# Two recurrent attention layers with expert gates on one core: gate and routing steps split and moved, the second experts one batch later

## The chip, the cores and the metric

One NeuronCore of one Trainium2 chip runs the whole program. The metric is the time of one execution in microseconds (us), taken on the device; the kernel before was run three times. A separate execution was profiled: its trace gives every row below. Engines are PE (TensorE), DVE (VectorE), ACT (ScalarE), POOL (GpSimd) and SP (SyncE, which here only issues DMAs).

## The reference, cut to what matters

`x` is 8 batches of 512 tokens of width 128. Two layers follow each other, each adds a product of two branches to `x`:

```python
xn = layernorm(x)
s = attn0(xn)                    # two 8-head attentions on 64 columns each (one on a Holt-smoothed copy),
                                 # two layernorms, a 128-512-128 relu MLP, a layernorm
g = silu(ffn0(xn))               # 16 experts, top 1, capacity 256 tokens, 128-512-128
x = x + s * g
xn = layernorm(x)
s = attn1(xn)                    # 16 heads of 8, causal, ALiBi
g = silu(ffn1(xn))               # 8 experts, top 2, 128-256-128 gated, no capacity limit
x = x + s * g
```

Attention is per batch. An expert layer needs the routing of all 4096 tokens before the first of its expert tiles can run, and the gate `g` of any batch needs all tiles. All of it is float32, with bfloat16 pieces in the scores (queries and keys are split into three bfloat16 parts).

## The kernel before, in words

**Stages.** `normalise0` normalises all tokens and scores the first gate. Then one software pipeline, `attention`, runs over steps b = -3 to 16 (`batches`, `plan`). Step b computes scores and softmax of batch b (batches 0 to 7 are layer 0, 8 to 15 layer 1), the row maxima of batch b+1, loads and projections of batches b+2 and b+3, and what is left of batches b-1 and b-2. Two blocks of expert tiles stand between steps: `experts0` (16 tiles) at the start of b = 1, and `experts1` (40 tiles of 256 slots) at the start of b = MIX1 = 11.

**Units and places.** A step of layer 0 has 64 units, one of layer 1 has 40. A unit is one bank of scores of batch b (PE L483, three banks in a ring, ACT takes the exponential, L642 to L646) and one bank of products for the maxima of batch b+1 (PE L491, another ring of three banks, DVE reduces it, L727 to L736). So PE can be three units ahead of ACT or DVE, and no more. The units are spread over 32 places, and at each place the tables `MISC` (every batch; by layer) and `EXTRA` (named b) name further steps. All five engines walk the same list in the same order, each doing its part of a step; semaphores with counted values are the only other order. All further PE products go through one bank, `ps_misc`, which the next step may claim only when the last has been read.

**Steps the change touches.**
- `q` and `k` (places 4 and 6; 3 and 5 in layer 1): PE projects, ACT writes `whole["q"]` or `whole["k"]` (L666), POOL splits it into three bfloat16 parts (L829 to L832, four instructions), SP writes these to DRAM. ACT waits before L666 until *all* splits so far are done.
- `gather`: POOL issues 4 (layer 0) or 8 (layer 1) indirect DMAs that fetch expert rows (L868). `gate`: POOL weighs them (L877 or L879 to L881), ACT takes the tanh (L679). `mix`: DVE makes `gz` (L783), POOL multiplies with the attention result and adds `x` (L892, L893), SP stores (L439).
- `choose`, `count`, `weigh` in b = ROUTE1 = 9: the second routing on DVE, 50-odd small dependent instructions (L903 to L907, L1478 to L1515, L1523 to L1527), in two blocks with a PE product between them.
- `send` (L1552): POOL issues 64 indirect DMAs that scatter the tokens to their slots in `sent1`, 24 in b = 9, 40 in b = 10. The tiles' first loads wait for all 64.
- `experts0.send_pool(2)`, on POOL's queue at the start of b = 1, ends with a wait for the DMAs that fill `sent1` with zeros (7 MB, issued by SP behind the last expert store).
- In b = 8, the first of layer 1, batch 7 still runs its layer-0 rest: `proj` and `gather` at place 7, `ln1` at 9 (POOL L839 to L846), `yT` at 15, `ff1` from 16, `ff2` at 23, `mix` at 28.
- Layer-1 batches 8 to 15 are mixed two in b = 11, two in b = 12, and one each in b = 13 to 16; step 16 has no units.

Of the kernel before, what the change touches and what calls it, by code (L numbers as in the profile page):

```python
# [15 lines left out]
P = 128  # L16
# [113 lines left out]
MIX1 = NB + 3  # L130
# [12 lines left out]
    1: {0: [("zT", 2)], 2: [("shift", 0, 1)], 3: [("q", 2)], 4: [("norm", -1, QT - 1)], 5: [("k", 2)], 7: [("onT", -1)],  # L143
        8: [("v", 1), ("load", 3)], 12: [("norm", 0, 0)], 16: [("fetch", 2, 0)], 17: [("proj", -1)], 19: [("shift", 1, 0)], 20: [("norm", 0, 1)],
        28: [("norm", 0, 2)]},
}

EXTRA = {
    ROUTE1: {12: [("choose", 0)], 14: [("count", 0)], 15: [("send", 0, 0)], 20: [("weigh", 0)]},
    ROUTE1 + 1: {7: [("send", 0, 1)], 18: [("send", 0, 2)]},  # L150
    MIX1: {0: [("loadx", -3), ("gather", -3)], 10: [("gate", -3)], 14: [("mix", -3)],
           15: [("loadx", -2), ("gather", -2)], 26: [("gate", -2)], 30: [("mix", -2)]},
    MIX1 + 1: {0: [("loadx", -2), ("gather", -2)], 10: [("gate", -2)], 14: [("mix", -2)],
               17: [("loadx", -1), ("gather", -1)], 26: [("gate", -1)], 30: [("mix", -1)]},
    **{b: {8: [("loadx", -1), ("gather", -1)], 24: [("gate", -1)], 30: [("mix", -1)]} for b in range(MIX1 + 2, STREAM + 1)},
}
# [46 lines left out]
def plan(b):  # L203
# [13 lines left out]
    def misc(place):  # L217
        for k in range(2):
            for step in MISC[k].get(place, []):
                if live(step[1]) and layer(step[1]) == k:  # L220
                    if step[0] == "fetch":
                        fetch(*step[1:])
                    else:
                        add(*step)
# [53 lines left out]
def adds(step):  # L278
# [5 lines left out]
    if name == "fetch":  # L284
# [34 lines left out]
def attention(nc, const, psum, banks, strips, late, work, dram, weights, routes, out, experts_of):  # L319


    with ExitStack() as ctx:
# [18 lines left out]
        neg_max = sb("neg_max", [P, 2, NG, QT])  # L341
        neg_block = sb("neg_block", [P, 2, NG, QT * QT])
# [6 lines left out]
        resid = [sb(f"resid{i}", [P, QT, D]) for i in range(2)]  # L349
# [30 lines left out]
        with nc.Block() as block:  # L380

            @block.sync
            def _(sp):
                n = Tally(adds)
                for b, steps in batches():
# [4 lines left out]
                    for step in steps:  # L390
# [1275 lines left out]
```

## Time and profile before

| | us |
|---|---|
| median of 3 runs | 1276.57 (1275.53 to 1281.41) |
| profiled execution | 1285.47 |
| its span, first to last instruction | 1283.5 |
| PE busy / DVE / ACT / POOL | 1049.2 / 776.5 / 656.6 / 541.2 |
| mean granted TensorE clock | 0.926 of full |

In slices of the span a busy share of PE near 0.9 stands for both steps at full rate and stretches at half clock, so the granted clock is to be read beside it. Starts of the steps, taken as the first exponential of a batch: b = 1 at 242.6, b = 2 at 316.8, b = 8 at 708.9, b = 9 at 771.8, b = 10 at 836.8, b = 11 at 1031.5, b = 12 at 1082.5, b = 13 at 1137.3, b = 14 at 1182.9, b = 15 at 1222.0; its last exponential ends at 1256.5. The expert tiles of layer 1 run from 908.9 to about 1030.

### The profile page before, as it was taken

The page shows a single profiled execution, that of the slowest core. Times are in us where ns is not written, and L with a number is a line of the kernel's source. Part 1 is how long each engine was busy: PE and PEld are TensorE (multiplying, and loading weights), DVE is VectorE, ACT ScalarE, POOL GpSimd, SP SyncE. Part 2 cuts the span into 40 slices and gives each one's busy share as a digit, 9 for nine tenths or more (in the row PEclk, how much of TensorE's full clock was granted, in tenths as well). Part 3 has the DMA queues.
Part 4 walks back from the last instruction along what each step waited for, and adds up shares of the span by engine and source line. Part 5 has one row for each costly group of instructions (what it writes and reads, how often), then busy time and mean ns, then how long its engine had stood idle before and what let it go on. Part 6 is the DMA issues. An engine that isn't in the chain of part 4 may idle for free.

```text
span 1283.5 us, 24573 instructions
## 1 busy us (share of the span) xinstructions
PE 1049.2 (82%) x8630; PEld 544.6 (42%) x8630; DVE 776.5 (60%) x1696; ACT 656.6 (51%) x1245; POOL 541.2 (42%) x568
## 2 busy tenths in 40 slices
PE   5349889969989898988899787784699978889982
PEld 5112249623333333333334444342589944434541
DVE  6359772457878787878755646754244446557710
ACT  1000662446767666667666545353244446556672
POOL 3154400062727272737363724477100056654344
PEclk9955999989999999999999989797799989899997
DMA  6345347661414141414141415244488843433211
GB/s 180 118 124 127 85 131 211 209 148 34 105 29 106 29 103 34 108 26 116 27 117 27 117 26 151 68 123 136 115 243 249 239 121 89 111 82 87 60 35 41
DMA packets 133348, 137.60 MB, mean 107 GB/s; under 512 B 14233, under 2 KB 115193, under 8 KB 133017
## 3 DMA queue, kind: packets, MB, share of 16 engines
q1 hardware_dynamic: 127096, 123.59, 37.1%
q0 software_dynamic: 6144, 12.60, 3.8%
q8 instruction: 66, 1.08, 0.4%
q14 instruction: 42, 0.34, 0.1%
HBM read 88.11 MB, written 54.58 MB: 111 GB/s over the span
## 4 chain that ended last, share of the span: by engine, by line
PE 51%; POOL 18%; DVE 9%; issue 6%; ACT 6%; DMA 4%; SPq 1%; POOLq 0%; ACTq 0%; DVEq 0%
PE ps_banks L526 7%; PE ps_banks L491 5%; PE ps_banks L1422 5%; PE ps_banks L483 5%; POOL sent L1552 5%; POOL tokens L868 4%; DVE a_neg_max L727 4%; PE ps_banks L602 3%; PE ps_banks L1435 2%; PE ps_banks L1217 2%; PE ps_banks L1203 2%; PE ps_banks L597 2%; PE ps_banks L545 2%; PE ps_banks L502 2%; PE ps_banks L566 2%
## 5 line engine op out<-in xcount | busy, mean ns | idle before, releaser
L727 DVE TENSOR_REDUCE a_neg_max<-ps_banks 128x1 f32<-128x512 f32 x512 | 325.8, 684 | 95.2 <-PE ps_banks L491 93.3
L642 ACT ACTIVATE a_probs<-ps_banks 128x512 f32<-128x512 f32 x512 | 282.9, 598 | 142.8 <-PE ps_banks L483 140.5
L491 PE MATMUL ps_banks<-k_strip,q_strip 51*128 51x128 bf16 (+2 forms) x1536 | 299.0, 296 | 42.9 <-DMA k_strip<-k_rows 21.6
L483 PE MATMUL ps_banks<-q_strip,k_strip 53*128 53x128 bf16 (+3 forms) x1408 | 283.7, 299 | 16.8 <-DVE a_neg_max L727 6.8
L644 ACT ACTIVATE a_probs<-ps_banks 128x512 f32<-128x512 f32 x256 | 146.9, 598 | 113.6 <-PE ps_banks L483 111.0
L491 PEld LDWEIGHTS ps_banks<-k_strip,q_strip 51*128 51x128 bf16 x1536 | 101.3, 95 | 233.9 <-ACT a_probs L642 109.7
L868 POOL DMA_INDIRECT tokens<-made,at x96 | 92.9, 968 | 155.5 <-DMA made<-work 127.9
L483 PEld LDWEIGHTS ps_banks<-q_strip,k_strip 53*128 53x128 bf16 x1408 | 94.8, 95 | 123.2 <-ACT a_probs L642 52.6
L729 DVE TENSOR_REDUCE a_neg_block<-ps_banks 128x4 f32<-128x512 f32 x128 | 87.2, 689 | 95.9 <-PE ps_banks L491 94.7
L526 PE MATMUL ps_banks<-a_probs,v_aug 128*32 128x512 f32 x1024 | 140.4, 621 | 0.0
L732 DVE TENSOR_REDUCE a_neg_block<-ps_banks 128x4 f32<-128x512 f32 x128 | 83.2, 683 | 31.8 <-PE ps_banks L491 31.5
L1535 DVE SCALAR_TENSOR_TENSOR work<-ps_banks,work 128x256 f32<-128x256 f32 x80 | 35.0, 480 | 87.4 <-ACT work L1458 58.0
L829 POOL CAST a_q_parts<-a_q_whole 128x512 bf16<-128x512 f32 x16 | 9.8, 612 | 182.3 <-DMA sent<-in_zeros 100.6
L1552 POOL DMA_INDIRECT sent<-tokens,at x64 | 61.5, 962 | 45.6 <-DVE at L1515 26.5
L1422 PE MATMUL ps_banks<-work 128*128 128x256 f32 x320 | 78.9, 391 | 1.3 <-DMA work<-in_pack 1.2
L808 POOL TENSOR_SCALAR a_ff_veps<-a_ff_moments 128x4 f32<-128x4 f32 x8 | 1.9, 235 | 161.8 <-DVE a_ff_moments L701 161.8
L1458 ACT ACTIVATE work<-ps_banks,work 128x256 f32<-128x256 f32 x80 | 33.6, 471 | 58.0 <-PE ps_banks L1422 58.0
L1422 PEld LDWEIGHTS ps_banks<-work 128*128 128x128 f32 x320 | 59.4, 196 | 9.1 <-DMA work<-in_pack 1.9
L502 PE MATMUL ps_banks<-mask_kq,ident_bf 128*128 128x512 bf16 x128 | 52.2, 408 | 7.8 <-ACT a_probs L644 6.3
L508 PE MATMUL ps_banks<-mask_qk,ident_bf 128*128 128x512 bf16 x128 | 51.7, 404 | 6.6 <-DVE a_neg_block L736 5.5
L545 PE MATMUL ps_banks<-consts,a_o_strip 128*128 128x128 f32 x256 | 42.6, 290 | 14.2 <-ACT a_o_strip L649 5.8
L736 DVE TENSOR_REDUCE a_neg_block<-ps_banks 128x4 f32<-128x512 f32 x64 | 42.1, 685 | 11.3 <-PE ps_banks L491 11.3
(223 smaller groups left out, 1691.1 us busy)
## 6 DMA issues: line engine op xcount, KB each, us to landing
work<-in_pack SPq DMA_DIRECT2D x40, 450.0 KB, 3.5
q_rows<-a_q_parts SPq DMA_DIRECT2D x96, 128.0 KB
k_rows<-a_k_parts SPq DMA_DIRECT2D x96, 128.0 KB
q_strip<-q_rows SPq DMA_DIRECT2D x64, 192.0 KB
k_strip<-k_rows SPq DMA_DIRECT2D x64, 192.0 KB
work<-in_w SPq DMA_DIRECT2D x32, 256.0 KB, 3.2
sent<-in_zeros SPq DMA_DIRECT2D x14, 512.0 KB, 7.9
work<-sent SPq DMA_DIRECT2D x56, 128.0 KB, 3.2
```

The costliest lines, as they stand in the source:

```text
L483: mm = pe.matmul(sbank[:, at:at + hi - lo], k_now[rows(js, ROW_END), slot, kt * P:(kt + 1) * P], q_now[rows(js, ROW_END), slot, lo:hi], st ...
L491: mm = pe.matmul(mbank[:, at:at + hi - lo], q_next[rows(jm, ROW_SHIFT), slot, qt * P:(qt + 1) * P], k_next[rows(jm, ROW_SHIFT), slot, lo:h ...
L502: pe.matmul(sbank, ident_bf[:], const["mask_kq"][:], start=True, stop=False)
L526: mm = pe.matmul(out_of[c], v_of[k][c], probs[group % 2][:, c, :], start=k == 0, stop=k == QT - 1)
L642: act.activation(probs[si // 4 % 2][:, si % 4, :], bank, ACT.Exp).then_inc(sems["probs"], 1)
L644: act.activation(probs[e // 4][:, e % 4, :], bank, ACT.Exp).then_inc(sems["probs"], 1)
L727: dve.tensor_reduce(neg_max[:, half, hd, qt:qt + 1], bank, AX.X, ALU.max, negate=True).then_inc(sems["max_out"], 1)
L729: dve.tensor_reduce(neg_block[:, half, hd, 0:QT * QT:QT], bank.rearrange("p (t n) -> p t n", t=QT), AX.X, ALU.max, negate=True).then_inc(s ...
L732: dve.tensor_reduce(neg_block[:, half, hd, :].rearrange("p (t k) -> p t k", t=QT)[:, 2:4, 1:3], bank.rearrange("p (t k n) -> p t k n", t=2 ...
L868: pool.indirect_dma_start(rows[:, t, :], None, moe[layer], bass.IndirectOffsetOnAxis(ap=routes[layer]["at"][i][:, QT * at + t:QT * at + t ...
L1422: mm = pe.matmul(hidden_bank(par, i)[:, c, :], pack[par][:, (i * FC1 + c) * P:(i * FC1 + c + 1) * P], rows_T[par][:], start=True, stop=True)
L1552: pool.indirect_dma_start(dram["sent1"], bass.IndirectOffsetOnAxis(ap=at[i][:, t:t + 1], axis=0), xn_all[:, t, :], None).then_inc(sems["se ...
```

## The change

It edits order and waits; the arithmetic stays, except that in layer 1's last batch DVE rather than POOL multiplies and adds.

- ACT, before writing `whole["q"]` or `whole["k"]`, waits for all splits but the last one (q and k alternate, so the last one read the other buffer).
- `gate` becomes `gate` (POOL), `tanh` (ACT) and `gz` (DVE) with places of their own; `mix` leaves its store to a step `store`.
- `choose` is cut in two, what was `count` in three (`count`, `place` 1, `place` 2), spread over places 12 to 24 of b = 9; `weigh` at 27.
- Sends go in 8 pieces of 8 DMAs: b = 9 place 28, b = 10 places 7, 15, 23, 30, b = 11 places 7, 15, 23. The wait for the zero fill stands before the first piece.
- MIX1 = 12: the expert tiles come after b = 11. Batches are mixed two per step in b = 12, 13 and 14; in b = 15 batch 14 is mixed, and batch 15 is gathered, gated and `gz` made. Attention results get three buffers. In b = 12 `proj` stands at 17.
- Step 16 has `final` in place of `proj`: the product, then two DVE instructions from PSUM and SBUF, then the store.
- In b = 8 batch 7's `gather` moves to 11, behind `ln1`; `yT` to 17, `ff1` to 18 to 21, `ff2` to 24, `mix` to 30.
- `neg_max` and `neg_block` are laid out so that `minus` reads them in order.

```diff
-MIX1 = NB + 3
+MIX1 = NB + 4
-        22: [("gate", -1), ("ff2a", -1)], 23: [("ff2", -1)], 25: [("ln2", -1)], 26: [("norm", 0, 2)], 28: [("mix", -1)]},
+        22: [("gate", -1), ("ff2a", -1)], 23: [("ff2", -1)], 24: [("tanh", -1)], 25: [("ln2", -1)], 26: [("norm", 0, 2), ("gz", -1)], 28: [("mix", -1)],
+        30: [("store", -1)]},
-    1: {... 7: [("onT", -1)], ... 17: [("proj", -1)], ...
+    1: {... 7: [("onT", -1)], ... 10: [("proj", -1)], ...
+LAST0 = {
+    **MISC[0], 7: [("proj", -1)], 11: [("gather", -1), ("logits", -2)], 15: [], 16: [("fetch", 2, 0)], 17: [("yT", -1)], 18: [("norm", 0, 1), ("ff1", -1, 0)],
+    19: [("ff1", -1, 1)], 20: [("ff1", -1, 2)], 21: [("shift", 1, 0), ("ff1", -1, 3)], 22: [("gate", -1)], 23: [("ff2a", -1)], 24: [("ff2", -1)], 25: [("tanh", -1), ("ln2", -1)],
+    26: [], 28: [("gz", -1)], 30: [("mix", -1)], 31: [("store", -1)],
+}
+def mixed(d, *at):
+    names = (("loadx", "gather"), ("gate",), ("tanh",), ("gz",), ("mix",), ("store",))
...
 EXTRA = {
-    ROUTE1: {12: [("choose", 0)], 14: [("count", 0)], 15: [("send", 0, 0)], 20: [("weigh", 0)]},
-    ROUTE1 + 1: {7: [("send", 0, 1)], 18: [("send", 0, 2)]},
-    MIX1: {0: [("loadx", -3), ("gather", -3)], 10: [("gate", -3)], 14: [("mix", -3)],
-           15: [("loadx", -2), ("gather", -2)], 26: [("gate", -2)], 30: [("mix", -2)]},
-    MIX1 + 1: {0: ... -2 ..., 17: [("loadx", -1), ("gather", -1)], 26: [("gate", -1)], 30: [("mix", -1)]},
-    **{b: {8: [("loadx", -1), ("gather", -1)], 24: [("gate", -1)], 30: [("mix", -1)]} for b in range(MIX1 + 2, STREAM + 1)},
+    ROUTE1: {12: [("choose", 0, 0)], 15: [("choose", 0, 1)], 18: [("count", 0)], 21: [("place", 0, 1)], 24: [("place", 0, 2)],
+             27: [("weigh", 0)], 28: [("send", 0, 0)]},
+    ROUTE1 + 1: {7: [("send", 0, 1)], 15: [("send", 0, 2)], 23: [("send", 0, 3)], 30: [("send", 0, 4)]},
+    ROUTE1 + 2: {7: [("send", 0, 5)], 15: [("send", 0, 6)], 23: [("send", 0, 7)]},
+    **{MIX1 + i: merged(mixed(i - 4, 0, 8, 11, 13, 14, 17), mixed(i - 3, 15, 24, 27, 29, 30, 31), {17: [("proj", -1)]} if i == 0 else {}) for i in range(3)},
+    STREAM - 1: merged(mixed(-1, 0, 8, 11, 13, 14, 17), mixed(0, 18, 25, 28, 30)),
 }
...
-                            wait(act, sems["split"], n.at("split"))
+                            wait(act, sems["split"], n.at("split") - 1)
...
-                            wait(act, sems["x2"], n.at("x2"))
-                            act.activation(s1_out[par]...
+                            wait(act, sems["x2"], NB + at - 2)
+                            act.activation(s1_out[at % 3]...
...
+                        if name == "final":
+                            wait(dve, sems["misc"], n.at("misc") + 1)
+                            wait(dve, sems["gate_out"], n.at("gate_out"))
+                            dve.tensor_tensor(sg[:], ps_misc.rearrange("p (t d) -> p t d", t=QT), gz[:], ALU.mult).then_inc(sems["misc_free"], 1)
...
+                            dve.tensor_tensor(x2[:], sg[:], x_in[:], ALU.add).then_inc(sems["x2"], 1)
...
-            pool.wait_ge(sems["zeroed1"], 16 * zero_dmas(w, TILES1 * SLOTS1))
+    def zeroed_pool(pool):
+        pool.wait_ge(sems["zeroed1"], 16 * zero_dmas(w, TILES1 * SLOTS1))
```

## Rows read from the trace of the kernel before

**Rows 1.** Windows: busy us (xcount) of PE, PEld, DVE, ACT, POOL; granted clock, DMA share, GB/s.

```profile
708.90:771.80 62.90, 51.78 (x592) 28.56 (x594) 36.03 (x90) 32.13 (x58) 32.21 (x35) 0.95 0.32 73
...
771.80:836.80 65.00, 47.61 (x570) 24.83 (x570) 46.45 (x117) 29.03 (x55) 28.80 (x32) 0.87 0.44 112
836.80:882.50 45.70, 39.67 (x538) 21.07 (x530) 27.32 (x52) 26.79 (x50) 35.72 (x38) 0.96 0.55 145
882.50:908.90 26.40, 0.00 (x0) 0.00 (x1) 2.30 (x6) 1.24 (x3) 17.36 (x19) 0.55 0.23 78
908.90:1031.50 122.60, 119.99 (x734) 106.91 (x738) 51.96 (x121) 50.30 (x122) 0.00 (x0) 0.97 0.75 218
1031.50:1082.50 51.00, 41.38 (x540) 21.35 (x532) 28.66 (x52) 29.69 (x55) 31.50 (x32) 0.93 0.45 107
1082.50:1137.30 54.80, 44.01 (x549) 22.23 (x548) 30.55 (x57) 29.02 (x55) 34.18 (x34) 0.91 0.45 103
1137.30:1182.90 45.60, 41.09 (x550) 21.43 (x548) 29.44 (x55) 28.40 (x55) 20.66 (x21) 0.96 0.40 95
1182.90:1222.00 39.10, 36.68 (x541) 20.10 (x539) 29.31 (x56) 26.46 (x51) 13.57 (x13) 1.00 0.23 50
1222.00:1256.50 34.50, 29.90 (x384) 15.77 (x383) 5.33 (x15) 25.41 (x50) 13.74 (x14) 1.00 0.12 32
1256.50:1283.50 27.00, 3.97 (x40) 2.44 (x40) 1.24 (x3) 2.94 (x6) 15.86 (x15) 0.70 0.18 49
```

**Rows 2.** Windows, same columns: one PE stall, and the stretches behind three PE stalls.

```profile
258.00:266.30 8.30, 0.39 (x7) 0.09 (x3) 0.69 (x1) 0.78 (x2) 3.51 (x4) 0.65 0.91 184
266.30:272.00 5.70, 5.70 (x30) 3.78 (x30) 3.56 (x20) 2.85 (x6) 4.47 (x6) 0.61 0.45 121
...
738.90:745.00 6.10, 6.10 (x41) 2.70 (x42) 0.88 (x2) 1.29 (x3) 2.26 (x2) 0.50 0.00 0
...
804.60:810.70 6.10, 6.10 (x45) 1.95 (x45) 5.69 (x21) 1.59 (x4) 0.00 (x0) 0.56 0.01 3
```

**Rows 3.** Waits: engine line <- releaser: us in total, times, longest us.

```profile
ACT a_k_whole L666 <- POOL a_q_parts L832: 42.4, 15, 9.0
...
PE ps_banks L1409 <- DMA work<-sent: 26.4, 1, 26.4
```

**Rows 4.** Timeline of b = 1, POOL and ACT: start, us, instruction, [idle before <-releaser].

```profile
261.68 0.61 POOL L829 CAST a_q_parts<-a_q_whole 128x512 bf16<-128x512 f32 x1 [100.56 <-DMA sent<-in_zeros]
...
265.52 0.69 ACT L666 ACTIVATE a_k_whole<-ps_banks,bk 128x512 f32<-128x512 f32 x1 [9.01 <-POOL a_q_parts L832]
```

**Rows 5.** Timeline of PE, in b = 8 and in b = 11.

```profile
738.89 1.11 PE L593 MATMUL ps_banks<-consts,work 128*128 128x128 f32 x4 [4.14 <-POOL work L844]
...
1047.47 1.12 PE L582 MATMUL ps_banks<-consts,a_o_norm 128*128 128x128 f32 x4 [4.10 <-ACT a_k_whole L666]
```

**Rows 6.** Timeline of DVE in b = 9: the routing's first and last instruction.

```profile
798.66 0.42 DVE L903 TENSOR_REDUCE work<-logits 128x32 f32<-128x256 f32 x1
...
815.40 0.18 DVE L1515 CAST at<-work 128x32 uint32<-128x32 f32 x1
```

**Rows 7.** Timeline of ACT and POOL in b = 9: q, then sends 1, 24 and 64.

```profile
779.28 0.60 ACT L666 ACTIVATE a_q_whole<-ps_banks 128x512 f32<-128x512 f32 x1 [0.74 <-PE ps_banks L566]
...
816.41 1.14 POOL L1552 DMA_INDIRECT sent<-tokens,at  x1 [26.54 <-DVE at L1515]
...
845.65 0.95 POOL L1552 DMA_INDIRECT sent<-tokens,at  x1 [0.30 <-issue]
...
904.39 0.96 POOL L1552 DMA_INDIRECT sent<-tokens,at  x1 [0.30 <-issue]
```

**Rows 8.** Timeline of the end: the last PE product and the last addition.

```profile
1261.97 1.16 PE L587 MATMUL ps_banks<-wo,a_o_T 128*128 128x128 f32 x8 [0.69 <-ACT a_o_T L653]
...
1276.67 1.26 POOL L893 TENSOR_TENSOR work<-tokens,work 128x512 f32<-128x512 f32 x1
```

**Rows 9.** Source L761, a DVE addition from PSUM: count, ns least/median/most.

```profile
L761 DVE TENSOR_TENSOR tokens<-ps_banks,a_resid x8: 691/692/692, 268.4 to 724.3; 128x512 f32<-128x512 f32 x8
```

More of the change, by code:

```diff
@@ new lines, in mixed, with merged @@
+def mixed(d, *at):
+    names = (("loadx", "gather"), ("gate",), ("tanh",), ("gz",), ("mix",), ("store",))
+    places = {}
+    for place, steps in zip(at, names):
+        places.setdefault(place, []).extend((name, d) for name in steps)
+    return places
+def merged(*tables):
+    places = {}
+    for table in tables:
+        for place, steps in table.items():
+            places.setdefault(place, []).extend(steps)
+    return places
+EXTRA = {
+    ROUTE1: {12: [("choose", 0, 0)], 15: [("choose", 0, 1)], 18: [("count", 0)], 21: [("place", 0, 1)], 24: [("place", 0, 2)],
[4 more added lines that the diff above has]
+    STREAM - 1: merged(mixed(-1, 0, 8, 11, 13, 14, 17), mixed(0, 18, 25, 28, 30)),
@@ L218, in misc @@
         for k in range(2):
-            for step in MISC[k].get(place, []):
-                if live(step[1]) and layer(step[1]) == k:
+            for step in (LAST0 if b == NB and k == 0 else MISC[k]).get(place, []):
+                if not live(step[1]) or layer(step[1]) != k or step[0] == "proj" and b == MIX1:
+                    continue
+                if step[0] == "proj" and b == STREAM:
+                    add("final", -1)
+                else:
                     if step[0] == "fetch":
@@ L295, in adds @@
         "ln2": {"pool": 2, "s": 1}, "gather": {"rows": 16 * QT * (1 if layer == 0 else TOP)},
-        "gate": {"gate_in": 1, "gate_tanh": 1, "pool": 0 if layer == 0 else 1},
-        "mix": {"gate_out": 1, "pool": 1, "x2": 1, "x2_out": 16},
+        "gate": {"gate_in": 1, "pool": 0 if layer == 0 else 1}, "tanh": {"gate_tanh": 1}, "gz": {"gate_out": 1},
+        "mix": {"pool": 1, "x2": 1}, "store": {"x2_out": 16}, "final": {**both, "x2": 1, "x2_out": 16},
         "ln3a": {"dve": 1, "moments": 1, "rstd": 1, "pool": 1}, "ln3b": {"xn2": 1, "xn2_out": 16},
-        "choose": {}, "count": both, "weigh": {}, "send": {},
+        "choose": {}, "count": both, "place": {}, "weigh": {}, "send": {},
     }
@@ L1472, in linking, with choose_vector @@
         return link
-    def choose_vector(dve):
+    def choose_vector(dve, part):
         link = linking(dve)
         number = const["all"][:, C_EXP1:C_EXP1 + E1]
-        first_best(dve, link, logits[:], E1, number, best[0], flag, first, onehot[0])
-        link(dve.scalar_tensor_tensor(rest[:], onehot[0][:], MASK, logits[:], ALU.mult, ALU.add))
+        if part == 0:
+            first_best(dve, link, logits[:], E1, number, best[0], flag, first, onehot[0])
+            link(dve.scalar_tensor_tensor(rest[:], onehot[0][:], MASK, logits[:], ALU.mult, ALU.add))
+            return
         first_best(dve, link, rest[:], E1, number, best[1], flag, first, onehot[1])
@@ L1492, in place_vector, with tile_vector @@
         before, totals = (ps_misc[:, i * NT * E1:(i + 1) * NT * E1].rearrange(by_expert, e=E1) for i in range(2))
-        total = places(dve, link, last_read, before, totals, run, pos)
+        assert places(dve, link, last_read, before, totals, run, pos) is run[1]
+    def tile_vector(dve):
+        link = linking(dve)
+        total = run[1]
         link(dve.tensor_tensor(filled[:], total[:, NT - 1, :].unsqueeze(2).broadcast_to([P, E1, FILLS]),
@@ L1549, in send_pool @@
             pool.wait_ge(sems["slots"], 1)
-        for t in range(*SEND[part]):
+        for t in range(QT * part, QT * (part + 1)):
             for i in range(TOP):
```

69 lines of the change are left out of this document (39 added, 30 removed).

## The prediction

> **What bounds the kernel now.** I read the windows first, one for each step of the pipeline and each gap between stages [rows 1], and in them three things: how long the step is, how busy PE is, and what clock PE was granted. The layer-1 steps do almost the same work (the same 40 units; steps 9 to 13 also the same projections), so the best of them is a measure for the others. Step 13 takes 45.6 us with PE busy for 41.1; step 9 takes 65.0, step 11 takes 51.0 and step 12 takes 54.8. PE sets a layer-1 step where nothing disturbs it; the rest is stalls. DVE is the next engine: 29.4 us of 45.6 in step 13, but 46.5 of 65.0 in step 9, where the routing runs.
>
> Then the stretches behind stalls [rows 2]. After each stall PE runs at about half clock for some us: granted 0.61 over 5.7 us, 0.50 over 6.1 us, 0.56 over 6.1 us, that is the 1.2 GHz level instead of 2.4 for all or most of it. Work lost is (1 - clock) times length: 2.2, 3.0 and 2.7 us. So a stall of several us costs itself and 2 to 3 us more. By the same arithmetic step 13 lost (1 - 0.96) x 45.6 = 1.8 us, and an undisturbed layer-1 step is 45.6 - 1.8 = 43.8 us [rows 1].
>
> Last the waits and timelines, for what ends each stall: the zero fill (step 1), POOL's y (step 8), the splits by POOL (steps 9 to 12), the routing (step 9), the sends (before the tiles), and the gate at the end.
>
> **The change part by part.** All sums are in the profiled execution: span 1283.5, time 1285.5, against a median of 1276.6 (0.7% less).
>
> 1. *Zero fill.* In step 1 POOL's first split starts at 261.68 because it stood behind the wait for the zeros, and ACT's `k_whole` at 265.52 behind that split [rows 4]. PE is busy 0.39 us of 8.30: 7.9 lost, and 2.2 behind it at low clock [rows 2]. The wait moves in front of the first send, some 540 us later, when the zeros have long landed. POOL's other wait there, for the expert stores, stays, and the split parts are written to DRAM behind the zeros on the same queue; their readers come at place 16, twice as far into the step as place 7 where PE stood. Bounds: 0 (the stores are as late as the zeros) and 10.1. The DMA share of 0.91 in that window at 184 GB/s is the zero fill itself, not the stores, so I take 10.
>
> 2. *Own-buffer waits.* ACT waited 42.4 us in 15 places for a split [rows 3]; 9.0 are those of part 1. In layer 0 the wait is short and PE has up to three units in hand; I count nothing (bounds 0 and 3 in all). In layer 1 PE stood 4.10 us in step 11 for `k_whole` [rows 5], because POOL had put the eight gather DMAs ahead of the split; about as much in 12, half of it in 9 and 10. It is contained in the step lengths below. What is late next is POOL itself (parts 5 and 6).
>
> 3. *Step 8.* PE waits 4.14 us for y [rows 5] and then loses 3.0 at half clock [rows 2]. The four gather DMAs, 1.26 us each as the sends are [rows 7], now come after `ln1`, so y is ready about 5 us earlier and PE claims it two places later: the stall goes. In exchange `ff2` is one place later and with it the last x of layer 0, on which DVE waits at place 1 of step 9; a place is 2 us (62.9 / 32 [rows 1]), about what is gained elsewhere. Bounds 2 and 7.1; I take 6.5.
>
> 4. *Step 9, the routing.* It keeps all its instructions; only the blocks get smaller. The first block began at 798.66 and the last ended at 815.58 [rows 6], 16.9 us with three reductions in between; with `weigh` it is 17 us of DVE, as 46.5 - 29.4 says too [rows 1]. PE can be three units ahead, some 3 us. From place 12 on DVE has 17 + 20/32 x 29.4 = 35.4 us of work; PE has 20/32 x 43.8 = 27.4. So DVE bounds the rest of this step, split or not, and small blocks only fill its idle time and avoid the long PE stalls with the slow clock behind them. The routing starts at 798.7 - 771.8 = 26.9 into the step, less 4 by part 2 (2.3 of stall, 1.7 behind it): 22.9. Add 35.4, 1.2 for DVE waiting for the count product behind which `shift` at place 19 must queue, less 2.5 by which PE is ahead at the end: 57 instead of 65.0. Bounds: 52 (the whole three units are in hand each time) and 65.
>
> 5. *The sends.* The slots are known after place 24: 22.9 + 15.9 + 12/32 x 29.4 + 1.2 = 51 into the step. By parts 1 and 3 step 9 starts at 771.8 - 16.5 = 755.3, so the slots are there at 806.3, and the first eight sends run to 816.4 at 1.26 each; this pace is the same among attention work (sends 1 to 24: 29.2 us for 23 steps) and alone (to send 64) [rows 7]. Step 10 starts at 812.3. From then POOL is never free: the next sends stand behind the splits, which need `q_whole`, 8.1 us into a step (779.88 - 771.8 [rows 7]): 820.4. In steps 10 and 11 POOL owes four splits, 4 us each (265.52 - 261.68 = 3.84 [rows 4]), 16 in all, and 56 sends, 70.6: done at 907.0. Before, send 64 ended at 905.35 and PE began the tiles at 908.9; with the same 3.5 us they now begin at 910.5. Steps 10 and 11 are 43.8 each and PE is done at 899.9: it waits 10.6 us where it waited 26.4 [rows 1, 3]. The splits of step 11 stand behind send piece 5 and end about 19 us into the step; their strips are fetched at place 16, 22 us in, and PE reads them in the next step: covered, by little on SP and by far on PE.
>
> 6. *After the tiles.* They take 122.6 us [rows 1], unchanged: step 12 starts at 1033.1. Steps 12 to 15 now mix seven batches and gate the eighth. POOL's load for a step with two: 34.2 busy as in step 12 before, 16 x 0.30 us between DMAs [rows 7], two landings of under 2 us: about 43 in 43.8 us. It just fits, and since `tanh` and `gz` are 3 to 5 places behind `gate`, ACT waits at `tanh` for 1 to 3 us, which the three banks mostly cover. I take step 12 at 44 (the step behind the tiles was shorter at its start), 13 at 45.5, 14 at 40 (39.1 before), 15 at 37.5 (34.5 before; now two gathers, and POOL's second gate comes late against its short places). Bounds: nothing for the gates (43.8 + 43.8 + 39.1 + 34.5 = 161.2) and what steps 11 and 12 showed (rival one); mine sum to 167.0.
>
> 7. *The end.* PE's last product ends at 1263.13 and the last addition at 1277.93 [rows 8]; between them lie gather, landing, gate, tanh, gz and mix. Now two DVE instructions of 0.69 [rows 9] follow the product: 1264.7, 13.2 less. From the last exponential to the end that is 27.0 - 13.2 = 13.8. It needs `gz` of batch 15 before that, for which step 15 has room. Bounds 9 and 13.5.
>
> 8. *Layout of the maxima, three result buffers, places in layer 0.* Two DVE instructions in a half get contiguous reads; DVE isn't the bound there. Nothing (bounds -2 and +2).
>
> The sum: 1033.1 + 167.0 + 13.8 = 1213.9, against 1283.5: **69.6 us less**. By source: zeros 10, step 8 6.5, step 9 8, step 10 1.9, wait for the sends 15.8, steps 11 to 13 18 (151.4 becomes 43.8 + 44 + 45.5 = 133.3), steps 14 and 15 -3.9, end 13.2. Profiled time 1285.5 - 69.6 = 1215.9, a factor of 0.946; on the median 1276.6 that is 1207.5.
>
> **A rule that speaks against it.** Of the 64 sends, 24 were issued beside attention with DVE at work, at 1.27 us, and the other 40, half of them with DVE idle, at (904.39 - 845.65 - 8 for the two splits between) / 40 = 1.27 [rows 7]. So DVE's work here costs the sends nothing. The Trainium skill says otherwise for some work ("SBUF — State Buffer", SBUF: two separate sides): a DVE instruction in a two-port mode locks GpSimd out, which then can't write the descriptors of its DMAs, 3.1 us against 0.62 in its example. By that rule more sends beside attention would be slower; the same page, under Who interferes with whom, exempts reductions, and by that the trace agrees. It is the last rival, priced from rows.
>
> **The rivals.**
>
> *One: the gates keep costing what they did.* For: steps 11 and 12 held two mixes each and took 51.0 and 54.8, and PE stood for `tanh` in both; POOL's 43 us of 43.8 leave nothing, so any lateness is carried on. Against: of their excess the larger part is the wait for the split, which goes, and `tanh` stood at the very place of `gate`. Then step 12 is 51.0, 13 is 54.8, 14 is 39.1 + 5, 15 is 34.5 + 9: 193.4 in place of 167.0, in all 1234.
>
> *Two: POOL is done in time and PE doesn't wait for the sends.* For: the wait is 10.6 us in a sum of 100 us, and a longer step 10 or 11 hides part of it; if the routing ends 5 us sooner, the sends do too. Against: POOL's sum has no guess in it but the slots' time. Then 10.6 less: 1197.
>
> *Three, on the other side: sends beside attention are slow.* All 56 that follow the first piece lie on POOL's chain to the tiles, now beside projections, splits and their DMAs. At x us each the end moves by 56 (x - 1.26): the gain is used up at x = 2.5, a time of 1277, and at 3 us each it is 1305. For it: nothing but that POOL's DMAs now share two whole steps with the rest. Against it: the even pace of both kinds of send [rows 7].
>
> *Four: the change doesn't take effect.* If a moved wait stands in the path again (the expert stores, `x2` before `loadx` on SP's queue), single terms of the sum fail, 10 to 20 us each; all of them don't.
>
> **How the numbers follow.** My forecast: 0.67, with a range of its own of 1198 to 1219 (parts 3, 4 and 6 by their bounds, not all at once). Rival one 0.15, rival two 0.10, three 0.03, four 0.05 (1220 to 1245). What a measurement of this kernel tells from no change is about 0.5%, 6 us. Faster 0.95, same 0.02, slower 0.03. The range 1195 to 1236 holds the first three cases; some 0.15 is left out.
>
> **What would show it.** In the profile after: PE busy through step 1 without the 7.9 us hole; step 8 near 56; step 9 near 57 with DVE busy about 46 of it, no PE stall over 2 us and a clock over 0.93; 64 sends at 1.26, the last about 907; a hole of about 10 us before the tiles (none: rival two; over 30: rival three); steps 12 and 13 at 44 to 46, with ACT waiting 1 to 3 us at the tanh (over 50: rival one); about 14 us from the last exponential to the end. I am wrong if step 9 stays at 65, if the pace of the sends changes, or if steps 12 to 15 sum to over 180.

## The result and the profile after

The changed kernel takes 1216.74 us (median of 4 runs, 1212.89 to 1225.2); the kernel before, run beside it, took 1278.99 (1275.53 to 1282.14). The ratio is 0.952, interval 0.946 to 0.959. The forecast was 1207.5, range 1195 to 1236: right in sign and about 9 us too low. Two further series gave 0.950 [0.948, 0.952] and 0.954 [0.949, 0.958]. Two single runs, of after_again at 1635.95 us and of last0_undone at 1597.63, had a mean granted clock of 0.56 and 0.64, and their medians below are those of the other three runs.

Windows of the profiled execution after (span 1223.4, time 1225.2), columns as in [rows 1]: step 1, steps 8 to 11, the hole before the tiles, the tiles, steps 12 to 15, the end. The tiles now stand behind step 11.

```profile
242.30:306.60 64.30, 56.72 (x368) 20.36 (x367) 49.13 (x102) 43.75 (x82) 29.96 (x30) 1.00 0.54 146
...
695.60:755.30 59.70, 52.30 (x592) 28.53 (x594) 34.83 (x90) 32.26 (x59) 29.52 (x33) 0.94 0.34 77
755.30:816.10 60.80, 48.87 (x566) 25.77 (x562) 45.69 (x118) 29.08 (x55) 21.30 (x24) 0.86 0.42 107
816.10:858.90 42.80, 39.44 (x552) 21.13 (x548) 28.50 (x53) 27.83 (x52) 30.00 (x33) 1.00 0.47 119
858.90:900.30 41.40, 38.45 (x538) 20.56 (x531) 27.64 (x53) 26.58 (x50) 32.87 (x36) 1.00 0.59 160
900.30:913.60 13.30, 0.00 (x0) 0.00 (x0) 2.32 (x6) 1.25 (x3) 7.67 (x8) 0.65 0.28 97
913.60:1033.70 120.10, 118.45 (x734) 105.84 (x738) 51.91 (x120) 50.26 (x121) 0.00 (x0) 0.98 0.75 223
1033.70:1081.80 48.10, 41.57 (x540) 21.36 (x539) 28.61 (x51) 29.67 (x55) 31.45 (x32) 0.93 0.46 114
1081.80:1129.00 47.20, 41.27 (x549) 21.31 (x548) 31.77 (x57) 28.89 (x55) 34.09 (x34) 0.96 0.48 114
1129.00:1169.60 40.60, 37.31 (x541) 19.99 (x540) 32.62 (x59) 27.03 (x52) 28.04 (x27) 1.00 0.32 74
1169.60:1209.50 39.90, 34.20 (x384) 17.69 (x383) 5.36 (x14) 26.00 (x51) 26.18 (x26) 0.85 0.20 54
1209.50:1223.40 13.90, 7.09 (x40) 4.20 (x40) 1.93 (x4) 1.66 (x3) 0.00 (x0) 0.50 0.07 19
```

The profiled execution is 8 us above the median, so the table sets a second profile of the same kernel (*after_3*, span 1215.2) beside it. Lengths are compared, not instants: what lies ahead of step 1 varied by 7 us from run to run (step 1 starts at 242.3 and at 235.0). The last column is the best version of the experiments. All in us.

| stretch | before [rows 1] | forecast | after | after_3 | best |
|---|---|---|---|---|---|
| step 8 | 62.9 | 56.4 | 59.7 | 56.7 | 56.7 |
| step 9 | 65.0 | 57 | 60.8 | 61.5 | 61.6 |
| steps 10, 11 | 45.7, 51.0 | 43.8, 43.8 | 42.8, 41.4 | 42.8, 41.4 | 42.8, 41.4 |
| hole before the tiles | 26.4 | 10.6 | 13.3 | 13.3 | 1.7 |
| tiles | 122.6 | 122.6 | 120.1 | 120.2 | 118.1 |
| steps 12 to 15 | 54.8, 45.6, 39.1, 34.5 | 44, 45.5, 40, 37.5 | 48.1, 47.2, 40.6, 39.9 | 47.7, 47.3, 40.7, 40.7 | 45.6, 44.8, 40.3, 32.9 |
| end | 27.0 | 13.8 | 13.9 | 13.9 | 14.8 |
| sum from step 8 | 574.6 | 515.0 | 527.8 | 526.2 | 500.7 |

Ahead of step 8 the change took off 13.0 us: 9.9 in step 1 (74.2 to 64.3) and 3.1 in steps 2 to 7 (392.1 to 389.0), of which only the first was forecast. From step 8 on the forecast was 11 to 13 us too low, most of it in steps 12 to 15. So the total was nearer than its terms, since gains that nobody had booked, 3.1 us in layer 0 and 2.5 in the tiles, cover part of the misses: that part is luck.

Two waits carry it (columns as in [rows 3]). The first answers to the 26.4 of [rows 3]; the second is ACT standing before the tanh until POOL has formed the gate's input.

```profile
PE ps_banks L1453 <- DMA work<-sent: 13.3, 1, 13.3
...
ACT tokens L710 <- POOL tokens L921: 11.4, 5, 3.5
```

The same in the timelines (columns as in [rows 4]): the first split of step 1, which answers to [rows 4]; the last of the 64 sends; the tanh in step 12; the last product and addition, which answer to [rows 8].

```profile
253.26 0.61 POOL L869 CAST a_q_parts<-a_q_whole 128x512 bf16<-128x512 f32 x1 [94.54 <-ACT a_q_whole L697]
...
909.15 0.96 POOL L1605 DMA_INDIRECT sent<-tokens,at  x1 [0.31 <-issue]
...
1057.62 0.63 ACT L710 ACTIVATE tokens<-tokens 128x512 f32<-128x512 f32 x1 [3.54 <-POOL tokens L921]
...
1217.12 2.07 PE L617 MATMUL ps_banks<-wo,a_o_T 128*128 128x128 f32 x8 [0.69 <-ACT a_o_T L684]
...
1219.95 0.69 DVE L823 TENSOR_TENSOR work<-tokens,work 128x512 f32<-128x512 f32 x1
```

The split no longer waits for the zeros, the last send ends at 910.1 (forecast 907.0), and from the last product to the last addition it is 1.5 us instead of 14.8.

### The profile page after: what moved, and what is told of

It reads as the page before. It is cut to its first block, busy times and chain, and to the rows that moved or that the text cites. A ratio compares the mean times of both kernels' runs of the same rounds, so it can differ in the third digit from the quotient of the medians.

```text
span 1223.4 us, 24580 instructions
## 1 busy us (share of the span) xinstructions
PE 1049.8 (86%) x8630; PEld 545.9 (45%) x8630; DVE 777.8 (64%) x1698; ACT 655.4 (54%) x1244; POOL 542.9 (44%) x566
## 4 chain that ended last, share of the span: by engine, by line
PE 53%; POOL 17%; DVE 10%; ACT 6%; issue 6%; DMA 3%; SPq 1%; POOLq 0%; ACTq 0%; DVEq 0%
PE ps_banks L556 7%; PE ps_banks L521 6%; PE ps_banks L1466 5%; PE ps_banks L513 5%; POOL sent L1605 4%; POOL tokens L908 4%; DVE a_neg_max L758 3%; PE ps_banks L632 3%; PE ps_banks L596 3%; PE ps_banks L1479 3%; PE ps_banks L1245 2%; PE ps_banks L1259 2%; PE ps_banks L627 2%; PE ps_banks L575 2%; PE ps_banks L584 2%
## 5 line engine op out<-in xcount | busy, mean ns | idle before, releaser
L760 DVE TENSOR_REDUCE a_neg_block<-ps_banks 128x4 f32<-128x512 f32 x128 | 86.9, 689 | 62.3 <-PE ps_banks L521 61.9
L763 DVE TENSOR_REDUCE a_neg_block<-ps_banks 128x4 f32<-128x512 f32 x128 | 83.5, 684 | 35.3 <-PE ps_banks L521 34.9
L1466 PEld LDWEIGHTS ps_banks<-work 128*128 128x128 f32 x320 | 58.7, 194 | 7.9 <-DMA work<-in_pack 0.9
L575 PE MATMUL ps_banks<-consts,a_o_strip 128*128 128x128 f32 x256 | 43.9, 297 | 13.3 <-ACT a_o_strip L680 5.1
L781 DVE RECIPROCAL a_o_den<-ps_banks 128x16 f32<-128x16 f32 x64 | 16.3, 255 | 56.4 <-PE ps_banks L575 55.6
```

Source lines behind the costliest of these rows:

```text
L575: mm = pe.transpose(ps_misc[:, t * P:(t + 1) * P], o_strip[arg % 2][:, t * P:(t + 1) * P], ident[:])
L760: dve.tensor_reduce(neg_block[:, half, :, hd, 0], bank.rearrange("p (t n) -> p t n", t=QT), AX.X, ALU.max, negate=True).then_inc(sems["max ...
L763: dve.tensor_reduce(neg_block[:, half, 2:4, hd, 1:3], bank.rearrange("p (t k n) -> p t k n", t=2, k=2), AX.X, ALU.max, negate=True).then_i ...
L1466: mm = pe.matmul(hidden_bank(par, i)[:, c, :], pack[par][:, (i * FC1 + c) * P:(i * FC1 + c + 1) * P], rows_T[par][:], start=True, stop=True)
```

## The experiments

Times are compared within a series only. The first series (after_again, split_all, routing_whole, tiles_early) and the third (after_3 and those behind it) have the kernel before at 1277.3 and 1278.7 us. In the second (zero_wait, last0_undone, gate_in_last_step, late_tanh) the kernel before took 1393.2 (see the last section), and the changed kernel itself was not run in it, so its runs are read by single steps, each against the others of the series.

**after_again**: no edit.

> The changed kernel as it is, as the measure for the three beside it on this chip. Expected: 1217 us, 0.952 of before; step 9 at 60.8 us, 13 us of PE waiting before the tiles, steps 12 to 15 at 48.0, 47.3, 40.6 and 39.9. If the time depends on how long PE sits at low clock, the span moves with the mean clock, by some 10 us for 0.015.

1214.27 us, ratio 0.950 [0.948, 0.952]. Step 8 takes 56.7, so the 59.7 of the first profile was that execution's. Steps 9, 10, 12 and 13 take 61.5, 42.8, 44.4, 47.2, the hole is 13.2. Steps 12 to 15 sum to 172.0, 3.8 less than in the first profile, nearly all of it in step 12: ACT waits there 1.57 us at the tanh and not 3.54, and PE stands 1.1 us and not 3.1.

**split_all**: ACT waits for both splits again before it writes the second.

```diff
-  wait(act, sems["split"], n.at("split") - 1)
+  wait(act, sems["split"], n.at("split"))
```

> The changed kernel with one edit taken back: ACT waits for all splits before it writes q or k. Theory: gathers and sends that POOL issues ahead of a split stop PE through this wait. Then PE stalls of 2 to 4 us with 2 us of low clock behind come back in steps 9 to 13: about 4 in steps 9 and 10, 6 in step 11 (POOL still has a send piece), 6.5 in 12 and 13, 3 over layer 0. Ten of those in steps 10 and 11 fall into the 13 us that PE waits for the sends anyway, so the time is about 20 longer, 1237. Rival: the three units in hand cover the wait once the sends are in pieces; then under 8 longer.

1233.35 us, 0.966 [0.962, 0.970]: 19 us slower than the changed kernel, as expected. The waits name it:

```profile
ACT a_k_whole L697 <- POOL a_q_parts L872: 40.7, 15, 6.8
...
PE ps_banks L612 <- ACT a_k_whole L697: 20.6, 5, 6.2
```

The 40.7 us are the 42.4 of [rows 3] again, but only 20.6 reach PE, in five places of steps 9 to 13. The second longest, in step 11:

```profile
874.61 1.11 PE L612 MATMUL ps_banks<-consts,a_o_norm 128*128 128x128 f32 x4 [5.96 <-ACT a_k_whole L697]
```

Step 9 takes 65.3, as before the change (65.0), step 11 takes 49.9 and step 13 51.1. So step 9 owes its 4 us to this one wait and nothing to the rest. Steps 9 to 13 together are 26 us longer than in after_again; since PE comes to the tiles later, the hole is 5.5 us instead of 13.2, and some 18 us of the difference are left. Ahead of step 9 the wait costs next to nothing: step 1 takes 64.3 (64.2 in after_again), steps 2 to 7 387.3 (387.5) and step 8 57.0 (56.7).

**routing_whole**: the routing in its three old blocks; the waits and the tiles as changed.

```diff
-  ROUTE1: {12: choose 0, 15: choose 1, 18: count, 21: place 1, 24: place 2, 27: weigh, 28: send 0},
+  ROUTE1: {12: choose 0, choose 1; 14: count, place 1, place 2; 15: send 0; 20: weigh, send 1; 26: send 2},
...                                   (the other five pieces: four in step 10, one in step 11)
```

> The changed kernel with the routing in two blocks again (choose whole at place 12, count and both place parts at 14, weigh at 20), and the first three send pieces at 15, 20, 26 of step 9, the rest at 7, 15, 23, 30 of step 10 and 7 of step 11. Theory: DVE's sum bounds step 9 in either form, and what sets the start of the tiles is when POOL gets the slots. Then step 9 stays at 61 with two stalls of 5 to 6 us, the slots are known 40 us into it instead of 53, the 64th send ends before PE does and the 13 us hole closes to 1 or 2: 1205. Rival, as the prediction had it: small blocks save 8 us of step 9. Then step 9 is 65 to 69 here and most of the 12 is lost again: 1212 to 1217.

1212.23 us, 0.947 [0.944, 0.950], 2 us faster than the changed kernel if anything, where 1205 was expected. Step 9 takes 61.6: PE stands twice for 6 us where it stood for 2.7, 4.0 and 1.7, and the step is as long. The sends end at 890.8 instead of 906.8, but the hole is still 6.6 us, though PE was done at 898.7. The queue of SP (columns as in [rows 4]) says why:

```profile
891.86 2.54 SPq L465 DMA_DIRECT2D q_strip<-a_shift  x4
895.84 4.13 SPq L1412 DMA_DIRECT2D work<-in_pack  x4
900.02 7.49 SPq L1415 DMA_DIRECT2D work<-sent  x6
```

Four weight packs are issued ahead of the token rows for which PE waits: a second floor, 6.6 us, right under the one of the sends. Nothing in the prediction named it.

**tiles_early**: the tiles in front of step 11, as before the change; the rest as changed.

```diff
-MIX1 = NB + 4
+MIX1 = NB + 3
...                                   (the last four pieces of the sends at place 30 of step 10, the mixes one step earlier)
```

> The changed kernel with the tiles of layer 1 after step 10 again (batches mixed two in steps 11 and 12, one in 13 and 14, 14 and the gate of 15 in step 15; all sends in steps 9 and 10). Theory: POOL's chain sets the tiles' start, one step later or not; without step 11's work over it PE idles. POOL ends two splits sooner: tiles start at 906 instead of 914 with 45 us of PE idle before them, and the step done later costs its 43 to 48: span about 1258, time 1252. Rival: the crowded steps with two mixes are what costs, and fewer of them give most of it back: under 1235.

1254.11 us, 0.980 [0.975, 0.984], as expected (1252).

```profile
PE ps_banks L1454 <- DMA work<-sent: 48.7, 1, 48.7
```

POOL has 56 sends and the splits left behind step 9, so with only one step of attention above them PE waits 48.7 us. The step by which the tiles come later is worth 40 us here, the largest single piece. That is its price beside the spread routing: before the change the tiles stood as early and the hole was 26.4 us, since the routing gave the slots sooner.

**zero_wait** (second series): the wait for the zeros back in step 1.

```diff
   experts0["send_pool"](pool, b + 1)
+  if b == 1: experts0["zeroed_pool"](pool)
```

> The changed kernel with POOL's wait for the zero fill back in step 1. Theory: PE stops there for POOL's split of q only if the next product has to wait for k, which with own-buffer waits it no longer does: ACT writes whole k while POOL still waits. So of the 10 us of the two edits together the wait alone costs little, 0 to 3, and step 1 stays under 67. Rival, as the prediction booked it: the wait costs 8 to 10 by itself, step 1 at 73 to 74, 1226.

1370.42 us, 0.982 [0.977, 0.988] of the kernel before in that series. Step 1 takes 73.3, in the three other kernels of the series 64.9 to 66.7. So the rival of this run held and not its theory. The first split and the product behind y:

```profile
270.04 0.61 POOL L871 CAST a_q_parts<-a_q_whole 128x512 bf16<-128x512 f32 x1 [111.43 <-DMA sent<-in_zeros]
...
288.15 1.26 POOL L886 TENSOR_TENSOR work<-work,be 128x512 f32<-128x512 f32 x1
```

```profile
289.47 1.11 PE L623 MATMUL ps_banks<-consts,work 128*128 128x128 f32 x4 [9.62 <-POOL work L886]
```

The price of about 8 us is near the 10 booked, but not by the road of [rows 4]: with the own-buffer wait `k_whole` is on time (ACT is idle 0.24 us before it), and the lateness stays in POOL's order (splits, gathers, `ln1`) and comes out at y.

**last0_undone** (second series): step 8 with layer 0's old places.

```diff
-  (LAST0 if b == NB and k == 0 else MISC[k])
+  MISC[k]
```

> The changed kernel with the table of layer 0 in step 8 as in the other steps (gather at 7, yT at 15, ff2 at 23, mix at 28). Theory: PE's stall for y of 4 us with 3 us of low clock behind it comes back, step 8 is 62 to 63 instead of 56.7, the time 6 longer, 1222. Rival: later ff2 and mix cost step 9 what step 8 gained; then the sum of steps 8 and 9 stays at 118.

1366.42 us, 0.980 [0.974, 0.985]. Step 8 takes 60.7; it takes 58.4 in late_tanh and gate_in_last_step and 63.6 in zero_wait, which have the new places. y is ready 29.6 us into the step, in late_tanh 24.6: the 5 us of the forecast. But PE waited only 0.79 us for it, since in this series it gets there later itself. The order of the gathers is shown; what it is worth isn't, here.

**gate_in_last_step** (second series): the last batch's gather, gate, tanh and product in the last step again; the gates of the others as changed.

```diff
-  STREAM - 1: merged(mixed(-1, 0, 8, 11, 13, 14, 17), mixed(0, 18, 25, 28, 30)),
+  STREAM - 1: mixed(-1, 0, 8, 11, 13, 14, 17),
+  STREAM: mixed(-1, 8, 24, 25, 26, 30, 31),
...
-  if step[0] == "proj" and b == STREAM:
+  if False:
```

> The changed kernel with the last batch's gather, gate and mix in step 16 again, behind its attention, and the product read by ACT. Theory: the end grows from 13.9 to 27 us as it was before the change, and step 15 gets back the 3.9 us stall that the second gate put in it: 9 to 10 us longer in all, 1226. Rival: POOL finishes the gathers early anyway, since its order holds nothing else; then under 5 longer.

1371.56 us, 0.984 [0.979, 0.990]. The last exponential lies 17.1 us ahead of the end, in zero_wait and last0_undone, which have the changed kernel's places there, 11.2. POOL at the end:

```profile
1342.38 1.28 POOL L922 TENSOR_TENSOR tokens<-tokens 128x512 f32<-128x512 f32 x1
1363.82 1.26 POOL L935 TENSOR_TENSOR tokens<-tokens,a_resid 128x512 f32<-128x512 f32 x1 [20.16 <-DVE tokens L816]
1365.16 1.26 POOL L936 TENSOR_TENSOR work<-tokens,work 128x512 f32<-128x512 f32 x1
```

The gather and the gate's input were done 18 us before the last product, though the code has them in the step behind: POOL had nothing ahead of them. Before the change the mix of batch 14 at place 30 held POOL until the end. From the product's end to the last addition it is 4.6 us, 3 more than in the changed kernel; the end as a whole is 5.9 longer. So the theory's 13 us more at the end did not come, and its rival held in kind: 7 to 10 of the 13.2 us of part 7 come from freeing POOL's order. That it is the earlier mix that frees it is read from the queue, not tried by itself.

**late_tanh** (second series): each tanh at least two places behind its gate.

```diff
-  mixed(i - 4, 0, 8, 11, 13, 14, 17), mixed(i - 3, 15, 24, 27, 29, 30, 31)
+  mixed(i - 4, 0, 8, 13, 14, 15, 17), mixed(i - 3, 15, 24, 28, 29, 30, 31)
-  mixed(-1, 0, 8, 11, 13, 14, 17), mixed(0, 18, 25, 28, 30)
+  mixed(-1, 0, 8, 15, 16, 17, 18), mixed(0, 18, 25, 31, 31)
```

> The changed kernel with the tanh of the gates later: in steps 12 to 14 at place 13 instead of 11 (gz 14, mix 15) and at 28 instead of 27, in step 15 at 15 (gz 16, mix 17) and at 31. Theory: the 8.8 us by which steps 12 to 15 were over the forecast are ACT standing at a tanh for POOL's gate, with PE stalls of 3.1, 2.4, 1.2 and 3.9 us and low clock behind them. Then these stalls go, the four steps sum to 167 to 169 instead of 172 to 176, and the time is 6 to 8 less, 1209. Rival: POOL's load of some 43 us in each step is the bound; then a stall of the same size turns up elsewhere and the time stays at 1216.

1357.73 us, 0.975 [0.971, 0.980], the lowest of its series. It says nothing of the tanh, because PE stands for its own instructions in every layer-1 step of this series, and the changed kernel was not run beside it. The question went to the third series.

**after_3**: no edit, the anchor of the third series.

> The changed kernel as it is, beside the kernel before once more: the anchor for the three kernels that follow it on this chip. Expected 0.952 of the time before and, if the engines keep their instruction supply, the span of 1217 with step 10 at 42.8, a hole of 13 us before the tiles, and stalls of 2 to 4 us in step 9 and of 2 to 3.5 us at the tanh in steps 12, 13 and 15.

1217.42 us, 0.954 [0.949, 0.958], as expected to 1 us.

**packs_early**: routing_whole, and the first four packs at the start of step 11 on SP.

```diff
+  ROUTE1 + 2: {0: [("packs", 0)], ...
   def tiles_sync(sp):
-      sp.wait_ge(sems["tiles"], 1)
-      for k in range(4):
-          weights(k, k)
       sp.wait_ge(sems["sent"], 16 * NT * TOP)
```

> The routing in three pieces as before the change, and the first four weight packs of the tiles loaded by SP at the start of step 11 instead of between step 11 and the tiles. Theory (the second floor under the tiles is SP's own order: after its last shift rows it issues four packs in 4.1 us and then six token loads of 1.25 us each, and only the second of these lets TensorE start): the token loads are issued about 5 us sooner, the hole before the tiles falls from 6.6 (the kernel with the whole routing alone) to 1 to 2 us, and the span is 5 us below that kernel's, which was 0.947 of the time before: 0.943. Rival (the hole is set by the flight of the token rows or by the scattering still being under way in memory): it stays at 6 us and the time at 0.947; the packs in the queue ahead of the writes of step 11 may even delay these and cost 1 to 4 us in step 12.

1204.19 us, 0.9405 [0.936, 0.945]. SP's queue (two places of it), and the hole:

```profile
856.75 3.71 SPq L1412 DMA_DIRECT2D work<-in_pack  x4
...
891.80 8.31 SPq L1422 DMA_DIRECT2D work<-sent  x6
```

```profile
PE ps_banks L1458 <- DVE a_neg_block L769: 1.7, 1, 1.7
```

The token rows are issued at 891.8, before PE is done at 896.6; the hole is 1.7 us and ends by DVE's last maxima. The theory holds, the rival (the flight of the rows) is excluded. It is 13 us below after_3.

**best**: packs_early with the places of late_tanh.

> The kernel above, and in steps 12 to 15 the tanh at least two places behind its gate (places 13 and 28 to 31 instead of 11 and 27), so that ScalarE, which works in order, doesn't stand before it while GpSimd works through the gate's products. Theory (ScalarE's 2 to 4 us at each tanh empty TensorE's ring, and the half clock behind the stall costs as much again): of the 11.4 us that the tanhs wait, most go, steps 12 to 15 fall from 176 to about 169 us, and the time is 0.937 to 0.94 of the time before. Rival (the steps 12 to 15 are set by DVE and by the low clock whatever the tanh does): the four steps stay within 2 us and the time is that of the kernel above.

1195.27 us, 0.936 [0.933, 0.939], 22 us below after_3, the fastest of all, and 9 us below packs_early (1194.23 to 1200.3 against 1199.77 to 1208.66; the profiles below are packs_early's second slowest run and best's fastest, 14 us apart). Its windows, steps 12 to 15 and the end:

```profile
1014.00:1059.60 45.60, 39.57 (x548) 21.07 (x548) 27.93 (x51) 28.66 (x52) 31.52 (x32) 1.00 0.49 121
1059.60:1104.40 44.80, 39.46 (x548) 21.14 (x548) 31.23 (x56) 28.83 (x55) 34.12 (x34) 1.00 0.51 120
1104.40:1144.70 40.30, 36.69 (x540) 20.23 (x540) 30.91 (x56) 26.95 (x52) 27.11 (x26) 1.00 0.32 75
1144.70:1177.60 32.90, 29.14 (x377) 15.59 (x378) 5.89 (x13) 25.33 (x49) 23.76 (x23) 1.00 0.23 64
1177.60:1192.40 14.80, 5.76 (x50) 3.62 (x47) 3.17 (x7) 3.29 (x6) 3.31 (x3) 0.76 0.08 23
```

The clock is 1.00 in all four steps (after: 0.93, 0.96, 1.00, 0.85), and they take 163.6 us; packs_early alone takes 173.2. ACT still waits at the tanh, 10.3 us in 5 places, but never over 2.4, where it was 3.5 and in packs_early 4.0. PE's own waits for ACT's exponentials in the four steps sum to 12 us in both. What differs is the clock: PE is busy 152.3 us in packs_early and 144.9 in best, 7.4 of the 9.6 us. It isn't the sum of the waits that costs, but the slow stretches behind some of them. Which waits bring these on isn't told by their length, as one stall of each kernel shows, packs_early first, with the windows behind it:

```profile
1094.06 0.28 PE L515 MATMUL ps_banks<-q_strip,k_strip 53*128 53x256 bf16 x1 [2.08 <-ACT a_probs L677]
...
1094.10:1098.10 4.00, 3.73 (x35) 1.55 (x38) 3.29 (x7) 2.45 (x5) 3.53 (x3) 0.61 0.16 46
```

```profile
1060.34 0.38 PE L534 MATMUL ps_banks<-mask_kq,ident_bf 128*128 128x512 bf16 x1 [2.23 <-ACT a_probs L677]
...
1060.30:1064.30 4.00, 3.96 (x50) 1.98 (x50) 3.90 (x8) 2.51 (x5) 3.53 (x3) 1.00 0.06 17
```

The shorter stall has the half clock behind it, the longer one hasn't; why is open.

**routing_next**: the whole routing one step later, in step 10.

```diff
-ROUTE1 = NB + 1
+ROUTE1 = NB + 2
...                                   (the seven later pieces of the sends in the step behind)
```

> The changed kernel with the whole of the routing one step later (choice, count, places, weights and the first piece of the sends in step 10, the other seven pieces in step 11), and the tiles where they are; nothing is left out. It will be slower, since 56 sends of 1.26 us need 70 us behind step 10: the hole before the tiles grows to 30 to 38 us. What it is for is step 9 without any routing. Theory (step 9's 61 us are 18 above step 10's because of the routing on VectorE): without it step 9 takes 44 to 50 and step 10 takes 55 to 60. Rival (step 9 is long because of the end of layer 0 that it also holds, its last layer norm, second transposes and logits, and the routing mostly fits beside attention): step 9 stays above 53 us and step 10 rises by less than 8.

1249.78 us, 0.978 [0.972, 0.984]. The hole before the tiles is 48.9 us, over the 30 to 38 expected. Steps 9, 10 and 11:

```profile
750.80:795.70 44.90, 41.17 (x564) 22.51 (x564) 30.49 (x64) 28.57 (x54) 16.05 (x18) 1.00 0.39 92
795.70:853.80 58.10, 45.79 (x554) 24.04 (x550) 44.10 (x108) 28.33 (x54) 11.61 (x13) 0.88 0.39 100
853.80:895.20 41.40, 38.43 (x538) 20.56 (x530) 27.32 (x52) 26.59 (x50) 29.68 (x33) 1.00 0.59 157
```

Against after_3 step 9 falls by 16.6 (61.5 to 44.9) and step 10 rises by 15.3 (42.8 to 58.1). The routing costs 15 to 17 us wherever it stands, nearly its own 17 us of DVE work; what is left of layer 0 costs step 9 2 us.

## Why the prediction was right or wrong

1. **Zero fill, −10: right in size.** Step 1 is 64.3 against 74.2. zero_wait prices the wait alone at 8, by y. By which road it comes depends on the other edit: with the own-buffer wait in place the stall of [rows 4] at `k_whole` is gone in any case; and with the zero wait moved, the old wait for both splits costs step 1 nothing (64.3 in split_all).

2. **Own-buffer waits, 0 in layer 0: right.** Steps 2 to 7 went from 392.1 to 389.0, and to 387.5 in after_again, but they take 387.3 with the old wait as well (split_all). So these 3 to 5 us belong to part 8, the layout of the maxima and the places of layer 0, which was put at nothing with 2 as its bound; no run takes those back one by one, and which of them it is stays open. In layer 1 the wait is worth 18 to 19 us of time (split_all).

3. **Step 8, −6.5: right**, −6.2: 56.7 in after_again and in all profiles of the third series. y comes 5 us earlier in the step, as reckoned; the old wait for both splits would cost the step 0.3 (split_all), so about 5.9 are left for the new places and what part 8 names. last0_undone was to price the places and could not, since PE's slow issue hid the stall.

4. **Step 9, 57: wrong by 3.8.** Its claim that the step is as long "split or not" held (routing_whole). The routing starts 24.7 us in, not 22.9, which is 1.8 of the miss. The other 2.0 are the sum from place 12 on: "Add 35.4, 1.2 for DVE waiting for the count product", less 2.5, makes 34.1, and it took 36.1. The form of that sum failed more than its size: DVE doesn't bound the rest alone, since from 779.9 to 816.1 it is busy only 31.2 of 36.2 us, 4 less than the 35.4 booked, and idle for 5. PE's stalls are the other side:

```profile
783.57 0.38 PE L538 MATMUL ps_banks<-mask_qk,ident_bf 128*128 128x512 bf16 x1 [2.66 <-DVE a_neg_block L763]
794.73 0.38 PE L607 MATMUL ps_banks<-ident_bf,a_minus 128*16 128x128 bf16 x4 [4.16 <-DVE work L962]
```

The second is the `shift` of place 19: it queues in order behind the count product and needs the same PSUM bank, which DVE frees only after the 3.8 us of running sums. I put 1.2 there. In the whole stretch PE's clock was 0.76; as I read it, the maxima came late to DVE and each engine waited for the other in turn. The clock of 0.86 for the step, where I wanted "over 0.93", was the sign. The 4 us gained are the own-buffer wait's (split_all: 65.3).

5. **Sends and hole, 10.6: 13.3.** The account of POOL held: 64 sends at 1.26, slots at 808.4 (806.3 forecast), the last send at 910.1 (907.0), PE's start 3.5 us behind it. The 2.7 us more: the last send came 3.1 us later than forecast, with step 9, while PE, whose steps 10 and 11 were 3.4 us shorter together, was done only 0.4 later (900.3 against 899.9). What I missed is that the wait had a second floor: rival two has PE not waiting at all once the sends are in time, but then 6.6 of the 13.3 us would have stayed, because of SP's order.

6. **Steps 12 to 15, 167.0: wrong by 5 to 9** (172.0 in after_again, 175.8 in the first profile), the largest miss. I let three banks "mostly cover" the tanh's 1 to 3 us. Three of the five waits were 2.6 to 3.5 us, and the clock of steps 12, 13 and 15 was 0.93, 0.96 and 0.85; rival one had the right mechanism at a third of its price (176 against its 193). best shows it was the places: with the tanh at least two later (`gz` and `mix` moved with it) the four steps take 163.6, below the forecast, where packs_early takes 173.2. Filling POOL to about 43 of 43.8 us was no trouble: with the same POOL work (31.5 and 34.1 busy) step 13 takes 44.8.

7. **The end, −13.2: right**, 27.0 to 13.9. Its cause was named too narrowly: the gate also had to come out from behind batch 14's mix (gate_in_last_step).

Rival three (slow sends beside attention) is excluded by the even pace of 1.26 us: in steps 10 and 11 DVE is busy 28.5 of 42.8 and 27.6 of 41.4 us and POOL's sends are as fast as alone. In these two steps 52.7 of DVE's 58.7 us by instruction are reductions. The Trainium skill ("SBUF — State Buffer", Who interferes with whom) exempts reductions from the lock between the two engines, and the trace agrees; the lock itself, which it states for two-port modes, isn't put to the test by such work. Also not booked: the tiles, 2.5 us shorter. In best they are 4.5 shorter, with the clock at 1.00 over them instead of 0.97 and 0.98: behind a hole of 1.7 us they start at full clock.

## What to carry to other kernels

An engine that works in order should meet a handoff late enough that it finds it done. Two places later gave 9 us. PE stood as long in sum, but the half clock behind its stalls was gone, and that was the larger part of the gain; the length of a single stall didn't tell whether it would come. When a wait is shortened, look for the next floor under it: here the sends (26 to 13), then SP's order of loads (6.6), then DVE (1.7); each has its row in the queue of the engine that issues the load. And splitting work that an engine must do anyway moves its holes, not its sum: three stalls of 2 to 4 us cost as much as two of 6.

## What the runs showed of the hardware

In the second series the kernel before ran 9% slower (1393.2 against 1277.3 and 1278.7). The record gives the same chip number for it as for the first series, so whether this is another chip or another condition of one chip isn't known. It isn't the duration of the instructions: an exponential took 598 ns in all series, a send 1.26 us. PE stood between matmuls with nothing to wait for. From late_tanh, a wait summed over the whole run, and the windows of steps 10 and 11:

```profile
PE ps_banks L560 <- issue: 51.5, 54, 3.1
```

```profile
834.00:919.00 85.00, 49.12 (x539) 24.01 (x544) 29.20 (x56) 28.01 (x53) 37.75 (x40) 0.72 0.25 66
919.00:993.00 74.00, 48.41 (x540) 23.69 (x546) 29.12 (x55) 28.07 (x53) 30.10 (x32) 0.77 0.35 93
```

These two take 85 and 74 us where the other series have 43 and 41, with single gaps of 1.73, 2.43 and 3.1 us in rows of many small matmuls; the layer-0 steps take 63 to 68 in all. It looks like the supply of PE's instructions, but no run tells what limits it. There the hole before the tiles is 2.6 us, since steps of 85 and 74 us hide the sends anyway, and the four kernels run there, each one edit away from the changed one, are 1.6 to 2.5% faster than the kernel before, against 5% for the changed kernel in the other series: how much a hidden wait costs depends on how slow the cover is.

SP's loads of token rows mostly take 0.37 us each to issue in the tiles' loop, but 1.25 each in the six that come in a row ahead of it (7.49 us in routing_whole). Why was not tried.
